# A MoE and attention kernel: half of the token blocks turned by VectorE in 32 by 32 squares

## The chip, the cores and the metric

The kernel runs on one core of a Trainium2 chip. The metric is the device time of one execution in microseconds (us). Before the change it is 405.93 us, the median of 3 runs.

## What is computed

x has 4 sequences of 512 tokens, 256 wide, float32: 2,048 tokens. It is normalised (xn), and the output is x plus attention(xn) plus a mixture of experts on xn:

```python
xn = _layernorm(x, axis=-1)
x = x + _L0_attn_ref(xn, Wq, Wk, Wv, Wo, bo) + _L0_ffn_ref(xn, router_w, router_bias, wg, wu, wd, swg, swu, swd)
# in _L0_ffn_ref, flat = xn as (2048, 256), E = 64 experts, F = 64, K = 4:
_, topk_idx = jax.lax.top_k(logits + router_bias, K)
g = jax.nn.silu(jnp.einsum('nd,edf->nef', flat, wg))
u = jnp.einsum('nd,edf->nef', flat, wu)
routed = jnp.einsum('ne,nef,efd->nd', comb, g * u, wd)
```

Each token goes to 4 of 64 experts; comb holds their weights. Two shared experts are added. Attention has 16 heads of 16 with a window of 64 and one key and value head.

## The kernel before, in words

Attention runs first, over NT = 16 tiles of 128 tokens, each engine with its own list of work written out by hand, tied by semaphores. In the meantime GpSimd scatters each normalised row to the HBM tensor `xs_d`, sorted by expert, once for each of its four experts (8,192 row slots). These are XB = 64 blocks of 128 rows of 256 numbers. With rounding to whole blocks per expert there are at most NBLK = 127 blocks of work, in NGRP = 32 groups of GS = 4; the blocks of work past 64 read token blocks that are already there, since a block of rows can hold several experts' rows.

The matmul with the expert weights needs a block with the features on the partitions. So each block b is loaded to one of NX = 8 buffers `xrow` (`load_block`, L1683 to L1691, a DMA of 128 rows of 1,024 bytes issued by SyncE), turned, and laid into `xall`, where it stays. Turning is `turn` on three engines:
- TensorE (L613 to L625): waits for the load and for a free bank, transposes two halves of the block (even and odd features, `c::NC`) into bank 0 or 4, and raises `g_T`.
- VectorE (L1139 to L1154) copies the even blocks from the bank to `xall`, and ScalarE (L874 to L889) the odd ones.

The first 10 blocks (FIRST) are turned in the last part of attention, at 177 to 195 us of the span. After that comes the loop over groups G = 1 to 32. `turns_of(G)` gives the blocks 4G + 6 to 4G + 9 in two pairs. TensorE's order in G is `ups(G)` (L650, 8 matmuls of a group's four blocks, each with its own wait for the weights and for the turned block), the first pair of turns (L624), `down(G-1)` (L675), the second pair. ScalarE does `silu(G)` (L896), a turn, `copy_y(G-1)` (L908, two copies), a turn. VectorE does a turn, `hidden(G)` (L1284, two products), a turn. GpSimd copies the picked weights (L1519, L1537).

SyncE's queue is in order. At T = 15 it issues the blocks 0 to 7, then two loads of the last eight experts, then (L1737 to L1745) blocks 8 and 9, a store of base (`store_base`, L1681), blocks 10 to 13, a store of base, and then down-weight loads (L1667) by turns with blocks 14 to 17. In G it issues for each block b of `turns_of(G)` the load of block b + 8, which waits until b's turn has read the buffer (L1690), and then `store_y(G-1)` (L1754), which waits for ScalarE's copy. In G = 1 the last store of base comes between the loads and the store of y, and a load of experts comes behind it in G = 1 and 2. ScalarE's `copy_y(1)` waits for all stores of base (L903), and from G = 2 on for the landing of the store of y of two groups before (L905). TensorE's `down(G)` waits for the copies of y of group G - 2 (L669).

At G = 17 (OTHER_DOWN) GpSimd begins to use two `xrow` buffers for weights, after all turns (L1529).

Of the kernel before, what the change touches and what calls it, by code (L numbers as in the profile page):

```python
# [17 lines left out]
B, L, D = 4, 512, 256  # L18
# [7 lines left out]
P = 128  # L26
NT = B * L // P
TPB = L // P
NC = D // P
# [115 lines left out]
def build(nc, x, Wq, Wk, Wv, Wo, bo, router_w, router_bias, wg, wu, wd, swg, swu, swd, c32, c16, edges, w32, w16, out):  # L145
# [4 lines left out]
    s = {n: ctx.enter_context(nc.semaphore("s_" + n)) for n in SEMAPHORES}  # L150
# [10 lines left out]
    bank = [psum[:, i * 512:(i + 1) * 512] for i in range(8)]  # L161
# [4 lines left out]
    xall = sb("xall", [P, NT * TOPK * D])  # L166
# [8 lines left out]
    xs_d = nc.dram_tensor("xs_d", (NT * P * TOPK, D), f32, kind="Internal").ap()  # L175
# [79 lines left out]
    NX, NW = 8, 4  # L255
# [18 lines left out]
    XB = NT * TOPK  # L274
# [46 lines left out]
    FIRST = 10  # L321
# [25 lines left out]
    up_bank_of = lambda G: bank[1 + G % 2]  # L347

    y_banks = lambda G: ((bank[3], bank[5]), (bank[6], bank[7]))[G % 2]
    turn_bank = lambda b: bank[4 * (b % 2)]  # L350

    turned = lambda b: (s["gT_dve"] if b % 2 == 0 else s["gT_out"], b // 2 + 1)

    turns_of = lambda G: [[b for b in range(4 * G + 6 + 2 * k, 4 * G + 8 + 2 * k) if b < XB] for k in range(2)]

# [4 lines left out]
    def tensor(pe):  # L360
# [251 lines left out]

        def turn(b):  # L613
            pe.wait_ge(s[f"xrow{b % NX}"], (b // NX + 1) * 16)
            if b >= 2:
                sem, n = turned(b - 2)
                pe.wait_ge(sem, n)
            elif b == 0:
                pe.wait_ge(s["max"], XT(NT - 1))
            else:  # L620
                pe.wait_ge(s["q_out"], 2 * NT)
            o = turn_bank(b)
            for c in range(NC):
                ins = pe.transpose(o[:, c * P:(c + 1) * P], xrow[b % NX][:, c::NC], ident)  # L624
            ins.then_inc(s["g_T"], 1)  # L625

        def turns(lo, hi):
            for b in range(lo, hi):
                turn(b)


        block_reg = [[ctx.enter_context(pe.register(f"block{n}_{i}")) for i in range(GS)] for n in range(2)]
# [136 lines left out]
        for G in range(1, NGRP + 1):  # L769
            if G == NGRP - 1:  # L770

                hidden(0, 0)
                down(G - 1)
            if G < NGRP:
                find(G)
                ups(G)
            if G == 1:
                project_out(NT - 1)
            for b in turns_of(G)[0]:
                turn(b)  # L780
            if G == NGRP:
                hidden(0, 1)
            if G != NGRP - 1:
                down(G - 1)
            for b in turns_of(G)[1]:
                turn(b)

        pe.wait_ge(s["with_x"], NT)
# [3 lines left out]
    def scalar(act):  # L792
# [79 lines left out]
                act.activation(th[i % 2], gate_bank(i), ACT.Tanh, scale=0.5).then_inc(s["th"], 1)  # L872

        def turn(b):  # L874
            if b == 1:

                act.wait_ge(s["q_left"], 2 * NT)
                act.wait_ge(s["weighted"], QB * (NT - 2))
            elif b == FIRST + 1:
                act.wait_ge(s["k_T"], NT)  # L880
                act.wait_ge(s["q_T"], 2 * NT)
                act.wait_ge(s["proj"], NT)
                act.wait_ge(s["weighted"], QB * NT)
            elif b in (SCORES_AT, SCORES_AT + 1):
                act.wait_ge(s["by_key"], XT(NT - 1))
                act.wait_ge(s["a_T"], NT)
                act.wait_ge(s["attended"], NT)
            act.wait_ge(s["g_T"], b + 1)
            act.activation(xall[:, b * D:(b + 1) * D], turn_bank(b)[:, 0:D], ACT.Copy).then_inc(s["gT_out"], 1)  # L889

        def silu(G):
# [93 lines left out]

        scores(NT - 1, 0, 0)
        scores(NT - 1, 0, 1)
        turn(1)
# [3 lines left out]
        turn(3)  # L992
        attention(NT - 2)
        turn(5)
        turn(7)
        silu(0)
        attention(NT - 1)
        turn(9)

        for G in range(1, NGRP + 1):  # L1000
            if G == NGRP - 1:
                copy_y(G - 1)
            if G < NGRP:
                silu(G)
            for b in turns_of(G)[0][1:]:
                turn(b)
            if G != NGRP - 1:
                copy_y(G - 1)
            for b in turns_of(G)[1][1:]:
# [7 lines left out]
    def vector(dve):  # L1017
# [119 lines left out]
            dve.tensor_tensor(ob, bank[7][:, 0:D], x_in[b][:, t, :], ALU.add).then_inc(s["with_x"], 1)  # L1137

        def turn(b):  # L1139
            if b == 0:  # L1140
# [4 lines left out]
            elif b == FIRST:  # L1145
                dve.wait_ge(s["q_T"], 2 * NT)
                dve.wait_ge(s["proj"], NT)
                dve.wait_ge(s["weighted"], QB * NT)
            elif b in (SCORES_AT, SCORES_AT + 1):
                dve.wait_ge(s["by_key"], XT(NT - 1))  # L1150
                dve.wait_ge(s["a_T"], NT)
                dve.wait_ge(s["attended"], NT)
            dve.wait_ge(s["g_T"], b + 1)
            dve.tensor_copy(xall[:, b * D:(b + 1) * D], turn_bank(b)[:, 0:D]).then_inc(s["gT_dve"], 1)  # L1154

        route_n = [0]

# [225 lines left out]
            if T > 1 and T < NT - 1:  # L1383
                add_x(T - 2)

        turn(0)
        add_x(NT - 3)
        tokens(NT - 2)
        turn(2)
        output(NT - 1)  # L1390
        turn(4)
        add_x(NT - 2)
        tokens(NT - 1)
        turn(6)
        hidden(0)
        turn(8)

        for G in range(1, NGRP + 1):
            if G == 1:
                add_x(NT - 1)  # L1400
            for b in turns_of(G)[0][:1]:
# [5 lines left out]
            for b in turns_of(G)[1][:1]:  # L1407
                turn(b)

        copy_last_y(NGRP - 1)  # L1410
# [23 lines left out]
    def gpsimd(pool):  # L1434
# [87 lines left out]
        def pick_down(G):  # L1522
            if G == 0:

                pool.wait_ge(s["max_T"], NT)
            elif G < OTHER_DOWN:
                pool.wait_ge(s["down"], 2 * G)
            elif G == OTHER_DOWN:
                pool.wait_ge(s["g_T"], XB)  # L1529
# [34 lines left out]
        slots = scatter()  # L1564
# [46 lines left out]
    def sync(sp):  # L1611
# [71 lines left out]
        def load_block(b):  # L1683
            if b == 0:
                sp.wait_ge(s["scattered"], NT * TOPK * 16)
                sp.wait_ge(s["gate"], 1)
            if b == NX // 2:
                sp.wait_ge(s["wslice"], 1)
            if b >= NX:
                sp.wait_ge(s["g_T"], b - NX + 1)  # L1690
            sp.dma_start(xrow[b % NX], xs_d[b * P:(b + 1) * P, :]).then_inc(s[f"xrow{b % NX}"], 16)  # L1691

        def load_blocks(lo, hi):
            for b in range(lo, hi):
# [127 lines left out]
```

## Time and profile before

| | us |
|---|---|
| median of 3 runs | 405.93 |
| lowest, highest | 404.23, 411.58 |
| span of the profiled execution | 407.3 |
| TensorE busy | 354.1 |
| VectorE busy | 248.5 |
| ScalarE busy | 189.3 |
| GpSimd busy | 257.5 |

The span runs from the first to the last instruction of one profiled execution. PE is TensorE's matmuls and PEld its weight loads, DVE is VectorE, ACT ScalarE, POOL GpSimd, SP SyncE; a q behind a name is the engine's sequencer, which waits and issues DMAs. A duration of a DMA instruction on SPq is the time that the queue was held by issuing it, not that of the transfer.

### The profile page before, as it was taken

Reading aid. Unit: us, or ns where it says so; the run is one execution under the profiler, and the core shown is the slowest. Engines: PE = TensorE matmul, PEld = TensorE weight load, DVE = VectorE, ACT = ScalarE, POOL = GpSimd, SP = SyncE. Lnnn points to the kernel's source line nnn. Section 1 sums busy time; section 2 is a strip of 40 time slices with the busy share of each in tenths; the row PEclk is TensorE's granted clock in tenths of the full one; section 3 lists DMA queues with packets and bytes.
Section 4 is the critical chain, followed back from the end, with each engine's and each line's share of the span. In section 5 each row is a group of like instructions: output and inputs, shape, how many; then the busy total and the mean of one; then the engine's idle time right before and its main releaser. Section 6 shows DMA issues by size and latency. Waiting matters only on the chain.

```text
span 407.3 us, 8670 instructions
## 1 busy us (share of the span) xinstructions
PE 354.1 (87%) x2711; PEld 259.3 (64%) x2711; DVE 248.5 (61%) x717; ACT 189.3 (46%) x359; POOL 257.5 (63%) x522
## 2 busy tenths in 40 slices
PE   6698487988976899899999999999999997989753
PEld 3696355665654556448889999999974544545442
DVE  4668877877876878624554645454444419375676
ACT  3485667686766677533455555555532111010100
POOL 5677986777777665022446566877837757667560
PEclk9969989898999889957999999999999999999969
DMA  8940144444484446545988873577974324434341
GB/s 255 213 109 1 54 131 146 131 146 133 161 241 150 142 146 176 156 141 134 296 263 269 267 249 132 181 244 233 337 252 120 105 85 129 128 94 129 103 129 52
DMA packets 73037, 66.81 MB, mean 164 GB/s; under 512 B 9054, under 2 KB 68702, under 8 KB 72994
## 3 DMA queue, kind: packets, MB, share of 16 engines
q1 hardware_dynamic: 66433, 49.30, 40.8%
q0 software_dynamic: 6144, 16.79, 13.0%
q8 instruction: 23, 0.38, 0.4%
q10 hardware_dynamic: 416, 0.18, 0.2%
q14 instruction: 21, 0.16, 0.1%
HBM read 36.78 MB, written 29.23 MB: 162 GB/s over the span
## 4 chain that ended last, share of the span: by engine, by line
PE 64%; DVE 15%; another core or an unknown queue 8%; issue 5%; ACT 4%; DMA 2%; POOL 1%; SPq 0%; DVEq 0%; ACTq 0%; POOLq 0%
PE bank L650 14%; PE bank L675 8%; PE bank L589 8%; PE bank L515 5%; PE bank L624 4%; PE bank L540 4%; PE bank L609 4%; DVE xall L1092 3%; PE bank L436 3%; PE bank L491 3%; DVE xall L1324 3%; PE bank L417 3%; PE bank L523 2%; PE bank L458 1%
## 5 line engine op out<-in xcount | busy, mean ns | idle before, releaser
L1500 POOL DMA_INDIRECT xs_d<-spare,slot_i x64 | 64.2, 1003 | 29.3 <-PE bank L515 7.5
L1593 POOL DMA_INDIRECT wall<-y_d,y_row x64 | 61.4, 959 | 33.7 <-issue 18.3
L1519 POOL COPY spare<-wall 128x256 f32 x127 | 46.9, 400 | 29.9 <-PE bank L650 18.0
L650 PE MATMUL bank<-xall,spare 128*128 x508 | 64.1, 279 | 0.2
L1284 DVE TENSOR_TENSOR spare<-bank,spare 64x512 f32<-64x512 f32 (+1 forms) x64 | 44.1, 690 | 31.0 <-ACT spare L896 30.1
L650 PEld LDWEIGHTS bank<-xall,spare 128*128 128x128 f32 x508 | 59.4, 192 | 2.8 <-issue 0.7
L589 PE MATMUL bank<-xnT,xall 128*128 128x512 f32 x128 | 57.7, 594 | 0.5 <-issue 0.5
L908 ACT ACTIVATE spare<-bank 128x512 f32<-128x512 f32 (+1 forms) x62 | 33.7, 593 | 29.5 <-PE bank L675 17.9
L847 ACT ACTIVATE xall<-bank 98x1024 bf16<-98x1024 bf16 x32 | 32.7, 1021 | 22.6 <-PE bank L436 14.5
L855 ACT ACTIVATE xall<-bank 128x512 f32<-128x512 f32 x64 | 36.6, 601 | 12.5 <-PE bank L491 7.4
L609 PE MATMUL bank<-xall 128*128 128x256 f32 x128 | 32.0, 400 | 11.6 <-DVE xall L1309 8.3
L589 PEld LDWEIGHTS bank<-xnT,xall 128*128 128x128 f32 x128 | 24.0, 190 | 26.1 <-issue 25.4
L872 ACT ACTIVATE xall<-bank 128x512 f32<-128x512 f32 x16 | 9.2, 596 | 66.7 <-remote 41.9
L609 PEld LDWEIGHTS bank<-xall 128*128 128x128 f32 x128 | 25.2, 201 | 21.8 <-DVE xall L1309 10.1
L491 PE MATMUL bank<-xall,wdn 128*128 128x256 bf16 x128 | 24.2, 285 | 13.2 <-ACT xall L855 5.6
L1324 DVE SCALAR_TENSOR_TENSOR xall<-wall,gate,xall 128x256 f32<-128x256 f32 x64 | 31.1, 487 | 2.3
L1154 DVE COPY xall<-bank 128x256 f32<-128x256 f32 x32 | 13.6, 425 | 28.7 <-PE bank L624 28.3
L896 ACT ACTIVATE spare<-bank 64x512 f32<-64x512 f32 (+1 forms) x32 | 18.8, 586 | 25.8 <-PE bank L650 25.7
L838 ACT ACTIVATE xall<-xall 128x768 bf16<-128x768 f32 (+2 forms) x48 | 28.8, 624 | 2.4 <-POOL xall L1490 1.8
L1092 DVE TENSOR_REDUCE xall<-bank 128x4 f32<-128x316 f32 x64 | 28.2, 478 | 1.1 <-PE bank L458 0.5
L1298 DVE SCALAR_TENSOR_TENSOR xall<-xall,bank 128x512 f32<-128x512 f32 x16 | 10.9, 681 | 23.0 <-ACT xall L872 21.2
L1537 POOL COPY small<-wdn 128x128 f32 x24 | 7.0, 293 | 27.7 <-PE bank L675 24.2
(172 smaller groups left out, 656.0 us busy)
## 6 DMA issues: line engine op xcount, KB each, us to landing
y_d<-spare SPq DMA_DIRECT2D x31, 512.0 KB, 4.1
wall<-in_wg SPq DMA_DIRECT2D x16, 256.0 KB, 4.8
wall<-in_wu SPq DMA_DIRECT2D x16, 256.0 KB, 5.0
wdn<-in_wd SPq DMA_DIRECT2D x16, 256.0 KB, 4.5
spare<-xs_d SPq DMA_DIRECT2D x32, 128.0 KB, 2.8
small<-xs_d SPq DMA_DIRECT2D x32, 128.0 KB, 3.3
wall<-in_x SPq DMA_DIRECT2D x4, 512.0 KB, 5.7
base_d<-spare SPq DMA_DIRECT2D x16, 128.0 KB
```

What stands on the lines that cost most here:

```text
L491: ins = pe.matmul(bank[2 + e][:, i * 256:(i + 1) * 256], kN[0:KROWS, near_of(T), u, :], qS[0:KROWS, T % NQ, u, :, :].rearrange("p h q -> p ...
L589: ins = pe.matmul((gate_bank(i), up_bank(i))[half], wsh[:, c, half, ex, f0:f0 + P], xnT[:, c, g * GN:(g + 1) * GN], start=c == 0, stop=c = ...
L609: ins = pe.matmul(shared_bank(T), hs[T // GT % 2][:, k, t * P:(t + 1) * P], wshd[:, k, :], start=k == 0, stop=k == FC - 1)
L650: ins = pe.matmul(up_bank_of(G)[:, j * P:(j + 1) * P], wcur[i % NW][:, c * 2 * F:(c + 1) * 2 * F], x_half[c][:, bass.ds(o, P)], start=c == ...
L855: act.activation(probs[n % 2][:, e * 512:(e + 1) * 512], bank[2 + e][:, :], ACT.Exp).then_inc(s["exp"], 1)
L908: act.activation(yb[G % 2][:, 0:n, half * P:(half + 1) * P], o[:, 0:n * P].rearrange("p (j d) -> p j d", d=P), ACT.Copy).then_inc(s["y_out ...
L1092: dve.tensor_reduce(maxf[T % 2][:, w * 8 + 4 * e:w * 8 + 4 * e + 4], bank[e][:, 0:4 * NEAR].rearrange("p (g n) -> p g n", g=4), AX.X, ALU.max,
L1284: ins = dve.tensor_tensor(hT[G % 2][half, 0:n], up_bank_of(G)[F:P, 0:n], sg[0:F, 0:n], ALU.mult)
L1324: dve.scalar_tensor_tensor(a, yk[:, T, k, :], gate[:, T, k:k + 1], a, ALU.mult, ALU.add).then_inc(s["sum"], 1)
L1500: pool.indirect_dma_start(out=xs_d, out_offset=bass.IndirectOffsetOnAxis(ap=slot_i[:, T, k:k + 1], axis=0), in_=x_n[b][:, t, :], in_offset ...
L1519: pool.tensor_copy(wcur[i % NW].rearrange("p (c g f) -> p c g f", c=NC, g=2), wall[:, bass.ds(o, WE)].rearrange("p (g c f) -> p c g f", c= ...
L1593: pool.indirect_dma_start(out=yk[:, T, k, :], out_offset=None, in_=of, in_offset=bass.IndirectOffsetOnAxis(ap=y_row[:, T, k:k + 1], axis=0 ...
```

## The change

Even blocks are turned by TensorE and copied by ScalarE. Odd blocks are turned by VectorE alone, which transposes squares of 32 by 32 from `xrow` to `xall`. Since a square's rows must be on the right 32 partitions already, an odd block is loaded by four DMAs, each to 32 partitions, in pieces of 256 bytes (64 numbers of one row): 4 x 128 pieces a block. VectorE's transpose reads `xrow` with a step of two numbers, so that even and odd features come apart. The buffer of an odd block is free when VectorE has turned it. The turns stand at the places in each engine's order where the copies stood, with even and odd exchanged; a bank is used by every second even block.

```diff
+    on_pe = lambda b: b % 2 == 0
+    turn_bank = lambda b: bank[4 * (b // 2 % 2)]
+    turned = lambda b: (s["gT_out"] if on_pe(b) else s["gT_dve"], b // 2 + 1)
+    SQ = 32
+    row_read = lambda b: (s["g_T"] if on_pe(b) else s["gT_dve"], b // 2 + 1)
+    row_loads = lambda b: 16 * (1 if on_pe(b) else P // SQ)
+    both_halves = lambda v: v.rearrange("p (c e h) -> p h c e", c=P // SQ, h=NC)
...
 # TensorE
         def turn(b):
             pe.wait_ge(s[f"xrow{b % NX}"], (b // NX + 1) * 16)
-            if b >= 2:
-                sem, n = turned(b - 2)
+            if b >= 4:
+                sem, n = turned(b - 4)
                 pe.wait_ge(sem, n)
...
-            for b in turns_of(G)[0]:
+            for b in turns_of(G)[0][:1]:
                 turn(b)
...
 # ScalarE
-            act.wait_ge(s["g_T"], b + 1)
+            act.wait_ge(s["g_T"], b // 2 + 1)
...
 # VectorE
-            dve.wait_ge(s["g_T"], b + 1)
-            dve.tensor_copy(xall[:, b * D:(b + 1) * D], turn_bank(b)[:, 0:D]).then_inc(s["gT_dve"], 1)
+            dve.wait_ge(s[f"xrow{b % NX}"], (b // NX + 1) * row_loads(b))
+            dve.transpose(xall[:, b * D:(b + 1) * D].rearrange("p (h c j) -> p h c j", h=NC, j=SQ),
+                          both_halves(xrow[b % NX])).then_inc(s["gT_dve"], 1)
...
 # SyncE
             if b >= NX:
-                sp.wait_ge(s["g_T"], b - NX + 1)
-            sp.dma_start(xrow[b % NX], xs_d[b * P:(b + 1) * P, :]).then_inc(s[f"xrow{b % NX}"], 16)
+                sem, n = row_read(b - NX)
+                sp.wait_ge(sem, n)
+            slots = xs_d[b * P:(b + 1) * P, :]
+            if on_pe(b):
+                sp.dma_start(xrow[b % NX], slots).then_inc(s[f"xrow{b % NX}"], 16)
+            else:
+                for a in range(P // SQ):
+                    of = slice(a * NC * SQ, (a + 1) * NC * SQ)
+                    sp.dma_start(xrow[b % NX][a * SQ:(a + 1) * SQ, :].rearrange("j (c n) -> j c n", n=NC * SQ),
+                                 slots.rearrange("(c j) d -> j c d", j=SQ)[:, :, of]).then_inc(s[f"xrow{b % NX}"], 16)
```

The numbers of the blocks in ScalarE's and VectorE's lists (`turn(1)`, `turn(0)` and so on) and in the waits ahead of the first ones are exchanged to match.

## Rows read from the trace of the kernel before

**Rows 1.** The page, busy time of each engine: us, share of the span, instructions.
```profile
PE 354.1 (87%) x2711; PEld 259.3 (64%) x2711; DVE 248.5 (61%) x717; ACT 189.3 (46%) x359; POOL 257.5 (63%) x522
```

**Rows 2.** The chain that ended last: start us, us, who, how many.
```profile
196.78 4.56 DMA base_d<-spare
...
232.34 1.09 PE bank L675 x16
233.44 0.68 PE bank L624 x4
...
236.38 1.09 PE bank L675 x16
...
249.59 1.98 PE bank L650 x16
...
289.55 1.98 PE bank L650 x16
...
292.62 1.98 PE bank L650 x16
```

**Rows 3.** Groups by line from 213 to 245 us: busy, mean ns; idle before.
```profile
L1284 DVE TENSOR_TENSOR spare<-bank,spare 64x512 f32<-64x512 f32 x16 | 11.1, 694 | 0.4
...
L1154 DVE COPY xall<-bank 128x256 f32<-128x256 f32 x16 | 6.8, 425 | 14.3 <-PE bank L624 14.1
L889 ACT ACTIVATE xall<-bank 128x256 f32<-128x256 f32 x16 | 6.1, 382 | 0.0
L624 PE MATMUL bank<-cf,spare 128*128 128x128 f32 x32 | 5.6, 296 | 0.0
```

**Rows 4.** Timeline of SyncE's queue: start us, us held, line, tiles, how many.
```profile
169.44 1.80 SPq L1691 DMA_DIRECT2D spare<-xs_d  x4
...
173.19 0.43 SPq L1621 DMA_DIRECT2D wall<-in_wg  x1
...
183.58 0.80 SPq L1691 DMA_DIRECT2D spare<-xs_d  x2
...
188.72 1.29 SPq L1667 DMA_DIRECT2D wdn<-in_wd  x2
...
196.78 0.43 SPq L1681 DMA_DIRECT2D base_d<-spare  x1
...
229.87 0.80 SPq L1691 DMA_DIRECT2D small<-xs_d  x2
230.71 0.43 SPq L1754 DMA_DIRECT2D y_d<-spare  x1
...
240.21 0.87 SPq L1691 DMA_DIRECT2D small<-xs_d  x2
```

**Rows 5.** DMA lines by source: ns min/median/max, first and last start; L1691's landing.
```profile
L1691 SPq DMA_DIRECT2D spare<-xs_d x32: 319/430/951, 169.4 to 236.9; - x32
DMA to landing us min/median/max: 2.0/3.2/5.3
...
L1613 SPq DMA_DIRECT2D wall<-in_x x4: 447/502/602, 0.7 to 4.5; - x4
...
L1770 SPq DMA_DIRECT2D xall<-base_d x4: 507/528/817, 283.5 to 292.1; - x4
...
L1667 SPq DMA_DIRECT2D wdn<-in_wd x16: 608/642/1812, 108.5 to 191.8; - x16
...
L1629 SPq DMA_DIRECT2D xall<-in_Wk x1: 694/694/694, 2.5 to 2.5; - x1
```

**Rows 6.** DMA queues, packets, MB, share: ScalarE's (page), SyncE's (213 to 244 us).
```profile
q10 hardware_dynamic: 416, 0.18, 0.2%
...
q1 hardware_dynamic: 8476, 8.06, 82.5%
```

**Rows 7.** Engines busy by stretch; last: granted clock, DMA share, GB/s.
```profile
174.00:188.00 14.00, 14.00 (x63) 7.85 (x64) 3.76 (x9) 4.98 (x10) 1.14 (x5) 0.52 0.41 122
...
213.00:245.00 32.00, 31.98 (x314) 29.98 (x316) 17.33 (x32) 17.88 (x40) 19.34 (x64) 1.00 0.84 265
```

More of the change, by code:

```diff
@@ L349, in build @@
     y_banks = lambda G: ((bank[3], bank[5]), (bank[6], bank[7]))[G % 2]
-    turn_bank = lambda b: bank[4 * (b % 2)]
-    turned = lambda b: (s["gT_dve"] if b % 2 == 0 else s["gT_out"], b // 2 + 1)
+    on_pe = lambda b: b % 2 == 0
[5 more added lines that the diff above has]
+    both_halves = lambda v: v.rearrange("p (c e h) -> p h c e", c=P // SQ, h=NC)
     turns_of = lambda G: [[b for b in range(4 * G + 6 + 2 * k, 4 * G + 8 + 2 * k) if b < XB] for k in range(2)]
@@ L628, in turns @@
             for b in range(lo, hi):
-                turn(b)
+                if on_pe(b):
+                    turn(b)
         block_reg = [[ctx.enter_context(pe.register(f"block{n}_{i}")) for i in range(GS)] for n in range(2)]
@@ L784, in tensor @@
                 down(G - 1)
-            for b in turns_of(G)[1]:
+            for b in turns_of(G)[1][:1]:
                 turn(b)
@@ L874, in turn @@
         def turn(b):
-            if b == 1:
+            if b == 0:
                 act.wait_ge(s["q_left"], 2 * NT)
+                act.wait_ge(s["k_T"], NT)
                 act.wait_ge(s["weighted"], QB * (NT - 2))
-            elif b == FIRST + 1:
+            elif b == FIRST:
                 act.wait_ge(s["k_T"], NT)
@@ L987, in scalar @@
         scores(NT - 1, 0, 1)
-        turn(1)
+        turn(0)
         scores(NT - 1, 1, 0)
@@ L991, in scalar @@
         act.activation(unread[:, :], ident[:, 0:1], ACT.Silu)
-        turn(3)
+        turn(2)
         attention(NT - 2)
-        turn(5)
-        turn(7)
+        turn(4)
+        turn(6)
         silu(0)
         attention(NT - 1)
-        turn(9)
+        turn(8)
         for G in range(1, NGRP + 1):
@@ L1004, in scalar @@
                 silu(G)
-            for b in turns_of(G)[0][1:]:
+            for b in turns_of(G)[0][:1]:
                 turn(b)
@@ L1008, in scalar @@
                 copy_y(G - 1)
-            for b in turns_of(G)[1][1:]:
+            for b in turns_of(G)[1][:1]:
                 turn(b)
@@ L1139, in turn @@
         def turn(b):
-            if b == 0:
+            if b == 1:
                 dve.wait_ge(s["q_part"], 3 * NT)
@@ L1144, in turn @@
                 dve.wait_ge(s["weighted"], QB * (NT - 2))
-            elif b == FIRST:
+            elif b == FIRST + 1:
                 dve.wait_ge(s["q_T"], 2 * NT)
@@ L1384, in vector @@
                 add_x(T - 2)
-        turn(0)
+        turn(1)
         add_x(NT - 3)
         tokens(NT - 2)
-        turn(2)
+        turn(3)
         output(NT - 1)
-        turn(4)
+        turn(5)
         add_x(NT - 2)
         tokens(NT - 1)
-        turn(6)
+        turn(7)
         hidden(0)
-        turn(8)
+        turn(9)
         for G in range(1, NGRP + 1):
@@ L1400, in vector @@
                 add_x(NT - 1)
-            for b in turns_of(G)[0][:1]:
+            for b in turns_of(G)[0][1:]:
                 turn(b)
@@ L1406, in vector @@
                 hidden(G)
-            for b in turns_of(G)[1][:1]:
+            for b in turns_of(G)[1][1:]:
                 turn(b)
@@ L1528, in pick_down @@
             elif G == OTHER_DOWN:
-                pool.wait_ge(s["g_T"], XB)
+                pool.wait_ge(s["g_T"], XB // 2)
+                pool.wait_ge(s["gT_dve"], XB // 2)
             else:
@@ L1689, in load_block @@
             if b >= NX:
-                sp.wait_ge(s["g_T"], b - NX + 1)
-            sp.dma_start(xrow[b % NX], xs_d[b * P:(b + 1) * P, :]).then_inc(s[f"xrow{b % NX}"], 16)
+                sem, n = row_read(b - NX)
+                sp.wait_ge(sem, n)
+            slots = xs_d[b * P:(b + 1) * P, :]
+            if on_pe(b):
+                sp.dma_start(xrow[b % NX], slots).then_inc(s[f"xrow{b % NX}"], 16)
[4 more added lines that the diff above has]
+                                 slots.rearrange("(c j) d -> j c d", j=SQ)[:, :, of]).then_inc(s[f"xrow{b % NX}"], 16)
         def load_blocks(lo, hi):
```

## The prediction

> **What bounds the kernel now.** I read the page first: TensorE is busy for 87% of the span, so the first guess is that less work for TensorE is less time [rows 1]. The changed part is a small stretch, so I went to the chain that ended last. From 205 us to 249 us it is a strict round of TensorE lines, L675, L624, L650, L624, and one group of four blocks takes 236.38 - 232.34 = 4.04 us. From 249 us on, when all 64 blocks are turned, the same round without L624 takes 292.62 - 289.55 = 3.07 us [rows 2]. So TensorE sets the pace there, and four turned blocks cost it 0.97 us, 0.24 us each. The granted clock is 1.00 in this stretch (2.4 GHz) [rows 7].
>
> Then I asked who is next. In 213 to 245 us a VectorE copy L1154 takes 425 ns and a ScalarE copy L889 382 ns; both engines are mostly idle beside them [rows 3]. SyncE's queue issues everything else: per group four block loads (L1691) and one store of y (L1754). A pair of loads holds it 0.80 us, the store 0.43 us [rows 4], so about 2.1 of 4.04 us. The DMA engines are the busiest after TensorE: 0.84 of the same stretch [rows 7]. Both have little room, and the change puts work on just these two.
>
> **The change, part by part.**
>
> TensorE loses 32 of 64 turns: per group 2 x 0.24 = 0.49 us, which would make the round 3.55 us if TensorE stayed the bound.
>
> ScalarE does the same 32 copies as before, only of other blocks: nothing. Bank use is the same two banks with the same two turns between uses: nothing.
>
> VectorE exchanges 32 copies of 425 ns for 32 transposes of 256 elements per partition. Before shows no VectorE transpose. Below I take the copy's 0.43 us; it has the same element count. Above I let it grow until it would matter: VectorE's other work in a group is the 1.4 us of L1284 (two of 694 ns) [rows 3], so two transposes could take 2.2 us each before they filled the round of 5.8 us that comes out below. It isn't the bound at any value I believe.
>
> The DMA engines: the packets of 1,024 bytes take 0.825 x 16 x 31 us / 8476 = 48 ns each [rows 6]. A group moves 1,024 of them now. After, it moves 768 of them and 1,024 of 256 bytes. For these the nearest row is the ScalarE queue's 416 packets of 0.18 MB in all, 0.2% of 16 engines' 407.3 us, so about 31 ns each (24 to 39 by the rounding), taken where little else ran [rows 6]; the upper end is the 48 ns of a big one. Per group: (768 x 48 + 1024 x 31)/16 = 4.3 us, at the ends 3.8 and 5.4 us. So already the transfers alone would take back the 0.49 us. The Trainium skill (DMA: Bandwidth & Descriptors, Specifications) says the same from the other side: transfers under 512 bytes don't run at line rate. The trace has no load of 256-byte pieces beside full traffic that would test it.
>
> SyncE's queue: this is the step that decides. An odd block is now four DMAs, 128 in all where there were 32. Eight block loads in a row took 173.19 - 169.44 us = 3.75 us, so 0.47 us from one issue to the next, though the queue waited for nothing; a single one after a pause takes 0.32 us [rows 4, 5]. What a piece (32 partitions, three dimensions, 32 KB) costs the queue isn't in the trace. Below: 0.37 us, the shortest load plus the 0.05 us between issues. Above: 0.73 us, from the 0.69 us of L1629 [rows 5]. Between them stand the loads whose SBUF side is contiguous and whose DRAM side has three dimensions, as here: L1613 median 0.50 us, L1770 0.53 us, L1667 0.64 us [rows 5]. I take 0.51 + 0.04 = 0.55 us per piece, since L1613 and L1770 are nearest in layout. For all else 0.47 us.
>
> A group's issues then take 2 x 0.47 + 8 x 0.55 + 0.47 = 5.81 us, over TensorE's 3.55, the DMA engines' 4.3 and the 4.04 of before. The queue becomes the bound. Now in order of time, with each issue at its price:
> - From 169.44 us: blocks 0 to 7, 4 x 0.47 + 16 x 0.55 = 10.7 us, to 180.1; two expert loads, to 181.1; blocks 8 and 9, 2.67 us, to 183.7; a store of base, to 184.2. Blocks 1, 3, 5 and 7 still come before their turn, since the turns run from 178 to 189 us.
> - Blocks 10 to 13, 5.34 us, to 189.5 (their turns free the buffers from 183.58 on); the store of base to 190.0; two pairs of down-weight loads (1.29 us and a gap of 0.05 each [rows 4]) and blocks 14 to 17 (5.34 us), to 198.0; blocks 18 to 21, to 203.4.
> - The last store of base, to 203.8. It was issued at 196.78 us, and its landing is 4.56 us of the chain, since ScalarE's copy of y for group 1 waits for it [rows 2, 4]. It is 6.7 us late.
> - One expert load and the store of y, to 204.8; group 2, 5.34 + 0.94, to 211.1; groups 3 to 11, 9 x 5.81 = 52.3, to 263.4; in group 12 only blocks 62 and 63, 2.67, to 266.0. In before this last pair began at 240.21 [rows 4].
> - The last piece, issued at 265.5, lands 3.2 us later [rows 5], VectorE turns it in 0.43 us, and TensorE may use block 63 at 269.1 us. It used it three quarters into the run that began at 249.59, at 251.1 [rows 2]. That is 18.0 us late, after all turning is done. From there the round has no turn in it and is the one of before, so nothing is given back.
>
> Queued behind the slow issues are the stores of y; a store late keeps ScalarE from writing the buffer two groups on, ScalarE keeps TensorE from the banks. By the sums above this delay is about the same as that of the last block, so it isn't added.
>
> Sum: 0 for ScalarE, VectorE and the DMA engines (all under 5.81 us per group), TensorE's gain hidden, +18.0 us for the queue. The profiled execution spans 407.3 us; the median of the runs is 405.93, 1.4 us less, and I know nothing else around the span. 407.3 + 18.0 is 425.3 in that execution; 405.9 + 18.0 = 424 us for the median. I leave out the clock: in 174 to 188 us it was granted 0.52, after TensorE had gone idle for short times [rows 7], and here TensorE would be idle 2.3 us of every 5.8. At half speed its round is 7.1 us. It could cost some us more, a reason for a long upper side.
>
> **Rivals.**
> - *Faster, the other side.* The pieces are issued in under 0.27 us each; then 3 x 0.47 + 8 x 0.27 = 3.55 us, the queue keeps up, and if the small packets take no more engine time than their bytes (1,024 x 12 ns, a quarter of 48), the round falls to 3.55 us for 12 groups: 12 x 0.49 = -5.9 us, and five of the ten early turns, 5 x 0.24 = -1.2 us: 399 us. Against it: no issue in the trace is under 0.32 us. The Trainium skill leans this way (DMA: Bandwidth & Descriptors, Issuing engines are not separate DMA queues): the sequencer's time for a DMA is usually small beside the DMA. Here the row of eight loads shows 0.47 us each. Chance 0.05.
> - *The queue about keeps up, the DMA engines set the pace.* A piece costs 0.37 to 0.45 us. At 0.37 the last piece comes in time by the same sum, and the 4.3 us of the DMA engines over 10 groups are +2.6 us, less what the eight buffers lend: 404 to 411 us. Chance 0.13.
> - *Forecast: the queue bounds, pieces at 0.45 to 0.70 us.* Each 0.01 us of a piece is 128 x 0.01 = 1.3 us. At 0.47: 415 us (1 us of the gain goes into waits for turns). At 0.68, by L1667: 441 us. Chance 0.75.
> - *Worse.* Pieces at 0.73 us, 447 us, or TensorE at half clock for most of the stretch. Chance 0.07.
> - *A slow transpose:* over 2.2 us it would add to the round; nothing speaks for it. The Trainium skill (VectorE: DVE Perf Modes, The three transpose paths) has VectorE's blocks quicker than TensorE's turn. It would add nothing to the sum. It is inside the 0.07.
>
> **How the numbers follow.** About 2% can be told from no change here, 398 to 414 us. Faster by more: 0.05. Within: 0.13. Slower: 0.82. The range goes from 411 (the upper end of the second rival, leaving out it and the first) to 442 (L1667's price, leaving out the worst): 0.8.
>
> **What would show it.** SyncE's queue waiting for nothing from 185 to 265 us, L1691 with 160 issues (128 of them near 0.5 us); the round of L650 to L650 near 5.8 us with idle time of TensorE ahead of L624 and L650; the last base store issued near 203 us; L1154's place taken by a transpose near 0.43 us; the DMA share under 0.8. I am wrong if pieces cost the queue under 0.45 us, if idle waits of L1691 for turns remain, or if the round is bound by packets.

## The result, and the profile after

The changed kernel is slower, by the sign and inside the range that were forecast, and 10 us beyond the likeliest value.

| | before | after |
|---|---|---|
| median of 4 runs, side by side on one chip | 408.12 us (404.23 to 411.58) | 434.4 us (431.62 to 437.2) |
| ratio of the comparison | | 1.0721, 95% interval 1.0642 to 1.0801 |
| profiled execution | span 407.3 us | 437.2 us, span 435.9 us |

(The ratio compares runs in the chip's faster state alone, so it isn't the quotient of the medians, which is 1.064; the same goes for the ratios below.) Against the forecast of 424 us the median is 10.4 us up.

Lines have moved: L650 is now L657, L675 is L682, L624 is L630, and L1691 is split. Even blocks are issued at L1704, the pieces of odd blocks at L1709. VectorE's copy of L1154 is the transpose of L1162, the store of y is L1773, the store of base L1691.

The page of the changed kernel: busy time of each engine, and the shares of the chain that ended last.

```profile
PE 352.8 (81%) x2647; PEld 255.7 (59%) x2647; DVE 250.8 (58%) x717; ACT 188.7 (43%) x359; POOL 258.1 (59%) x522
...
PE 34%; SPq 16%; DVE 16%; another core or an unknown queue 11%; issue 9%; ACT 6%; DMA 5%; POOL 1%; DVEq 0%; ACTq 0%; POOLq 0%
SPq L1709 11%; PE bank L657 7%; PE bank L682 4%; PE bank L595 3%; DVE xall L1333 3%; PE bank L521 3%; SPq L1704 3%; PE bank L442 3%; DMA spare<-xs_d 2%; PE bank L615 2%; DMA small<-xs_d 2%; PE bank L546 2%; PE bank L423 2%; ACT xall L845 2%
```

TensorE has 64 instructions fewer than in [rows 1] and loses only 1.3 us of busy time. The engine totals barely move, so they don't tell where 28.6 us of span come from. The chain does: SyncE's queue, which had 0% of it in the kernel before, has 16%, and 11% of the span is the single line L1709 that issues the pieces.

The timeline of SyncE's queue after (start us, us held, line, tiles, how many), at the first load, around the last store of base, for one group of four blocks and for the last pair:

```profile
172.15 0.38 SPq L1704 DMA_DIRECT2D spare<-xs_d  x1
...
205.98 0.43 SPq L1691 DMA_DIRECT2D base_d<-spare  x1
...
206.93 0.57 SPq L1773 DMA_DIRECT2D y_d<-spare  x1
...
245.53 0.50 SPq L1704 DMA_DIRECT2D small<-xs_d  x1
246.08 2.42 SPq L1709 DMA_DIRECT2D small<-xs_d  x4
248.55 0.43 SPq L1704 DMA_DIRECT2D spare<-xs_d  x1
249.02 1.85 SPq L1709 DMA_DIRECT2D spare<-xs_d  x4
250.92 0.43 SPq L1773 DMA_DIRECT2D y_d<-spare  x1
251.40 0.50 SPq L1704 DMA_DIRECT2D spare<-xs_d  x1
...
269.37 0.50 SPq L1704 DMA_DIRECT2D small<-xs_d  x1
269.91 2.43 SPq L1709 DMA_DIRECT2D small<-xs_d  x4
```

Read it against [rows 4]. The sum of the durations and the 0.05 us between issues fill the time: from 245.53 to 251.40 the queue is without an instruction for no more than these gaps, and that is the new round, 5.87 us where it was 4.04. The last pair begins at 269.37 us where it began at 240.21.

The source view of the pieces (durations ns min/median/max), against [rows 5]:

```profile
L1709 SPq DMA_DIRECT2D spare<-xs_d x64: 317/432/1851, 172.6 to 266.0; - x64
L1709 SPq DMA_DIRECT2D small<-xs_d x64: 429/432/1692, 177.3 to 271.9; - x64
...
  DVE xall L1162: 44.7, 22
```

The source view of the transpose, against the copy in [rows 3]:

```profile
L1162 DVE STREAM_TRANSPOSE xall<-spare x16: 433/445/447, 178.4 to 267.9; 128x256 f32<-128x256 f32 x16
```

The third line of the first view says who waited for the pieces: VectorE's transposes, 44.7 us in all. VectorE is quick enough (445 ns); it stands and waits for its data.

The engines by stretch after (length; busy us and count of PE, PEld, DVE, ACT, POOL; last the granted clock, the DMA engines' busy share, GB/s), against [rows 7]:

```profile
174.00:188.00 14.00, 12.21 (x92) 7.55 (x90) 3.69 (x9) 6.82 (x14) 3.96 (x12) 1.00 0.57 153
188.00:213.00 25.00, 18.38 (x129) 16.75 (x130) 10.70 (x21) 7.46 (x18) 8.38 (x26) 0.80 0.65 162
213.00:265.00 52.00, 38.09 (x329) 32.57 (x328) 19.41 (x35) 17.73 (x42) 22.87 (x73) 0.96 0.62 176
```

TensorE is now busy for 38 of 52 us, and the DMA engines are at 0.62 where they were at 0.84. Nothing but the queue is full. ScalarE's copies of y (L916, L908 before) waited in these 52 us for stores of y to land, 30.3 us in all (busy, mean ns; idle before):

```profile
L916 ACT ACTIVATE spare<-bank 128x512 f32<-128x512 f32 x16 | 8.7, 595 | 30.3 <-DMA y_d<-spare 30.3
```

That is not a second bound: the stores stand in the same queue behind the pieces, and the queue itself never waited more than 0.4 us for a copy or a turn.

The chain after (start us, us, who, how many), from the landing of the last piece:

```profile
271.91 3.17 DMA small<-xs_d
...
278.06 1.98 PE bank L657 x16
...
281.13 1.98 PE bank L657 x16
```

Once block 63 is in, the round is 281.13 - 278.06 = 3.07 us, the same as in [rows 2]. The run of L657 that starts at 278.06 is the one that started at 252.66 before (249.59 + 3.07). So 25.4 us are lost by here.

### The profile page after: what moved, and what is told of

Same layout as the page of the kernel before. It is cut to its first block, busy times and chain, and to the rows that moved or that the text cites. A ratio compares the mean times of both kernels' runs of the same rounds, so it can differ in the third digit from the quotient of the medians.

```text
span 435.9 us, 8608 instructions
## 1 busy us (share of the span) xinstructions
PE 352.8 (81%) x2647; PEld 255.7 (59%) x2647; DVE 250.8 (58%) x717; ACT 188.7 (43%) x359; POOL 258.1 (59%) x522
## 4 chain that ended last, share of the span: by engine, by line
PE 34%; SPq 16%; DVE 16%; another core or an unknown queue 11%; issue 9%; ACT 6%; DMA 5%; POOL 1%; DVEq 0%; ACTq 0%; POOLq 0%
SPq L1709 11%; PE bank L657 7%; PE bank L682 4%; PE bank L595 3%; DVE xall L1333 3%; PE bank L521 3%; SPq L1704 3%; PE bank L442 3%; DMA spare<-xs_d 2%; PE bank L615 2%; DMA small<-xs_d 2%; PE bank L546 2%; PE bank L423 2%; ACT xall L845 2%
## 5 line engine op out<-in xcount | busy, mean ns | idle before, releaser
L657 PE MATMUL bank<-xall,spare 128*128 x508 | 68.7, 291 | 1.5 <-issue 0.4
L657 PEld LDWEIGHTS bank<-xall,spare 128*128 128x128 f32 x508 | 63.1, 202 | 5.5 <-issue 3.3
L1293 DVE TENSOR_TENSOR spare<-bank,spare 64x512 f32<-64x512 f32 (+1 forms) x64 | 43.9, 685 | 33.9 <-ACT spare L904 33.3
L916 ACT ACTIVATE spare<-bank 128x512 f32<-128x512 f32 (+1 forms) x62 | 33.6, 593 | 63.6 <-DMA y_d<-spare 42.5
L615 PE MATMUL bank<-xall 128*128 128x256 f32 x128 | 32.9, 408 | 13.3 <-issue 8.7
L442 PE MATMUL bank<-cb,xall 128*98 128x128 bf16 x256 | 21.3, 230 | 0.2 <-ACT xall L854 0.2
```

Of the source, the lines that this page charges most:

```text
L442: ins = pe.transpose(o[0:SROWS + MROWS, h, :], qrow[T % 2][:, 8 * i + h, :], identb)
L615: ins = pe.matmul(shared_bank(T), hs[T // GT % 2][:, k, t * P:(t + 1) * P], wshd[:, k, :], start=k == 0, stop=k == FC - 1)
L657: ins = pe.matmul(up_bank_of(G)[:, j * P:(j + 1) * P], wcur[i % NW][:, c * 2 * F:(c + 1) * 2 * F], x_half[c][:, bass.ds(o, P)], start=c == ...
L1293: ins = dve.tensor_tensor(hT[G % 2][half, 0:n], up_bank_of(G)[F:P, 0:n], sg[0:F, 0:n], ALU.mult)
```

## The experiments

A result is the ratio to the kernel before with its 95% interval. The chips differ: the kernel before takes 373.8 and 373.4 us on the chips of the first eight runs (four each) and 407.8 us on that of the last four. Each ratio is against runs of the kernel before on the same chip.

The first question was what of the change costs: the number of issues, the small packets, or both.

**e1_split: only the issues.** The kernel before, with odd blocks loaded by four DMAs of 32 whole rows. No small packets, and TensorE still turns all blocks.

```diff
-            sp.dma_start(xrow[b % NX], xs_d[b * P:(b + 1) * P, :])...
+                for a in range(4):
+                    sp.dma_start(xrow[b % NX][32 * a:32 * a + 32, :],
+                                 xs_d[b * P + 32 * a:b * P + 32 * a + 32, :])...
```

> The kernel before, but each odd block is loaded by four DMAs of 32 whole rows (1,024-byte pieces); TensorE turns all blocks as before. So it has the number of issues of the change (160 for 64 blocks) and nothing else of it. Theory 'queue' (SyncE's queue is held 0.47 us by each issue): a group takes 11 issues, 5.2 us, and about 0.5 us more around the store of y as in the changed kernel, so 5.7 to 5.9 us a round where it was 4.04; +24 to +30 us, ratio 1.06 to 1.075. Rival 'packets' (256-byte pieces fill the DMA engines or land late): there are none, so the ratio is 0.99 to 1.01. Rival 'VectorE' (the transpose holds the buffers): also 0.99 to 1.01.

Measured: 400.82 us against 373.81, ratio 1.0748 (1.0688 to 1.0808). SyncE's queue in this kernel, timeline:

```profile
212.86 0.42 SPq L1759 DMA_DIRECT2D y_d<-spare  x1
213.33 0.50 SPq L1692 DMA_DIRECT2D small<-xs_d  x1
213.87 2.35 SPq L1695 DMA_DIRECT2D small<-xs_d  x4
216.26 0.42 SPq L1692 DMA_DIRECT2D spare<-xs_d  x1
216.73 1.83 SPq L1695 DMA_DIRECT2D spare<-xs_d  x4
218.61 0.42 SPq L1759 DMA_DIRECT2D y_d<-spare  x1
```

The round is 218.61 - 212.86 = 5.75 us, and the pattern is the one of after: 1.83 us for four issues, and 2.35 us for the four behind a store of y. So a loss of the change's size appears without a single small packet and without VectorE, and a piece's hold (0.42 us here, with 32 packets; 0.43 in the change, with 128 packets and three dimensions) doesn't come from its layout.

**e2_small: only the small packets.** The kernel before, with each odd block in one DMA of 256-byte pieces, each from another row than its neighbour.

```diff
+                sp.dma_start(xrow[b % NX].rearrange("p (c n) -> p c n", c=4),
+                             bass.AP(v.tensor, v.offset, [[D, P], [D + 64, 4], [1, 64]]))...
```

> The kernel before, but each odd block is loaded by one DMA of 512 pieces of 256 bytes (to 128 partitions; the pieces of a row come from neighbouring rows, so the odd blocks' data are mixed up and the output is not the reference's). It has the change's small packets and not its issues. Theory 'queue': 64 issues as before, ratio 0.995 to 1.015; the round stays at 4.04 us or goes to at most 4.3 us if the small packets cost the engines 31 ns. Rival 'packets': most of the loss is here, ratio over 1.04.

Measured: 1.0037 (0.9992 to 1.0083). The windows of this kernel:

```profile
190.00:220.00 30.00, 29.97 (x300) 27.97 (x299) 17.06 (x31) 16.36 (x38) 17.12 (x57) 1.00 0.90 261
```

and the source view of its small load:

```profile
L1696 SPq DMA_DIRECT2D spare<-xs_d x16: 362/434/828, 155.3 to 218.9; - x16
```

One DMA of 512 packets is held for 434 ns, as one of 128 packets is. What comes behind it is held a little longer, 0.51 us for the store of y here against 0.43 in the changed kernel:

```profile
195.91 0.43 SPq L1696 DMA_DIRECT2D small<-xs_d  x1
196.38 0.51 SPq L1760 DMA_DIRECT2D y_d<-spare  x1
```

The DMA share goes up to 0.90, and TensorE stays full. So small packets alone cost nothing that can be told from zero here.

**e3_plain: the gain without its price.** The changed kernel with plain loads of whole blocks, which leaves out putting each square on its 32 partitions. It shows what VectorE's half of the turns is worth when the loads come in time.

```diff
-    row_loads = lambda b: 16 * (1 if on_pe(b) else P // SQ)
+    row_loads = lambda b: 16
...
+            sp.dma_start(xrow[b % NX], slots).then_inc(s[f"xrow{b % NX}"], 16)
```

> The changed kernel with each odd block loaded by one plain DMA of whole rows; VectorE transposes what lies there, so the output is not the reference's (the squares of the odd blocks are at the wrong places). It has the change's work on the engines without its loads. Theory 'queue': SyncE has 64 issues, TensorE sets the round at 3.55 us, or the DMA engines at about 3.4; -4 to -8 us, ratio 0.98 to 0.99. Rival 'VectorE' (transposes or the exchanged order of turns hold the loop): slower than before, ratio over 1.02. Rival 'packets' says the same as 'queue' here.

Measured: 0.9767 (0.9714 to 0.982), a bit more than expected. Its chain:

```profile
199.70 1.09 PE bank L682 x16
...
203.26 1.09 PE bank L682 x16
```

and its windows:

```profile
180.00:212.00 32.00, 32.00 (x323) 29.75 (x323) 19.02 (x36) 20.20 (x46) 21.03 (x70) 1.00 0.99 323
```

The round is 203.26 - 199.70 = 3.56 us; the forecast's working had 3.55. That the DMA engines would be busy 0.99 of the time and still keep up had not been expected.

**e4_pairs: the same layout with fewer issues.** Blocks are taken in pairs: 4q and 4q+1 come in one DMA and TensorE turns them, 4q+2 and 4q+3 come in four DMAs that carry the pieces of both. Six issues a group with the store of y, not eleven, and VectorE still does half the turns.

```diff
+    on_pe = lambda b: b % 4 < 2
...
+            slots = xs_d[(b - 1) * P:(b + 1) * P, :]
+            if on_pe(b):
+                sp.dma_start(to(0, P).rearrange("p (i d) -> p i d", i=2), ...)
+            else:
+                for a in range(P // SQ):
+                    sp.dma_start(to(a * SQ, (a + 1) * SQ).rearrange("j (c n) -> j c n", n=NC * SQ),
+                                 slots.rearrange("(c j) d -> j c d", j=SQ)[:, :, of])...
```

> A correct kernel with the change's 256-byte pieces and VectorE's transposes, but half of the issues: blocks 4q and 4q+1 are TensorE's and come in one DMA, blocks 4q+2 and 4q+3 are VectorE's and come in four DMAs of 32 partitions and eight pieces each. A group has 6 issues where the changed kernel has 11. Theory 'queue': 6 x 0.47 + 0.5 = 3.3 us is under TensorE's 3.55 us and near the DMA engines' 3.6 us, so the round is 3.6 to 3.9 us; the time is -1 to -6 us against before, ratio 0.985 to 1.0. Rival 'packets': as many small packets as the change, so still at least half of its loss, ratio over 1.03.

Measured: 0.9978 (0.9937 to 1.0019). The loss of 7% is gone, and there is no gain that can be measured. Its windows:

```profile
180.00:212.00 32.00, 30.16 (x295) 27.42 (x293) 16.40 (x31) 18.41 (x44) 20.55 (x67) 1.00 0.95 267
```

and two pieces of its chain, with the turn of TensorE that the first one held up (in brackets its idle time before it):

```profile
175.41 5.71 DMA base_d<-spare
...
198.08 3.23 DMA spare<-xs_d
```

```profile
182.71 0.76 PE L632 MATMUL bank<-cf,small 128*128 128x128 f32 x4 [0.87 <-ACT xall L897]
```

The chain passes through the last store of base and, later, through two block loads. But TensorE had other work for most of that time: it was idle for 0.87 us at the store of base and for 32.00 - 30.16 = 1.8 us in the whole window. The DMA engines, at a share of 0.95, have little slack. From the first load to silu of group 14, the last with turns, it is 72.2 us here and 65.3 in e3; no run takes these 7 us apart.

**e5_base: take away that wait.** e4 with the last store of base issued ahead of the loads of blocks 18 to 21.

```diff
+            if G == 1:
+                store_base(NT - 1)
             for bs in turns_of(G):
...
-            if G == 1:
-                store_base(NT - 1)
```

> e4_pairs with the last store of base issued ahead of the loads of blocks 18 to 21 instead of behind them. In e4 TensorE stood still for about 5 us for the landing of this store. Theory 'queue': the store is issued about 2 us earlier, so -1 to -3 us against e4; ratio to the kernel before 0.988 to 0.997. Rival 'landing' (the DMA engines are full there, so it lands no earlier): as e4, 0.998.

Measured: 0.9962 (0.9923 to 1.0002), not to be told from e4. The 5 us of standing still in the expectation were read from the chain; TensorE's own idle time at that store was 0.87 us (above), so little was to be had.

**e6_y_on_act: one issue less a group, and none behind a store.** The changed kernel, with the stores of y issued by ScalarE.

```diff
+                act.dma_start(y_d[(G - 1) * GS * P:((G - 1) * GS + n) * P, :].rearrange("(j p) d -> p j d", p=P),
+                              yb[(G - 1) % 2][:, 0:n, :]).then_inc(s[f"y{(G - 1) % 2}"], 16)
...
-            store_y(G - 1)
+            if G - 1 >= NGRP - 2:
+                store_y(G - 1)
```

> The changed kernel with the stores of y (all but the last two) issued by ScalarE behind its copies and turns. The number of issues and packets is that of the change, but SyncE has 10 of a group's 11. Theory 'queue' (one sequencer's queue is the bound): the round goes from 5.87 to 4.7 to 5.0 us, and the ratio to before from 1.07 to 1.03 to 1.05. Rival 'shared' (what makes descriptors, or the DMA engines, is the bound for both queues together): no gain, over 1.06.

Measured: 1.0754 (1.0686 to 1.0822), a miss. SyncE's queue in this kernel; ScalarE issued a store of y at 219.43 and held 0.37 us for it:

```profile
216.79 1.89 SPq L1714 DMA_DIRECT2D spare<-xs_d  x4
218.73 0.43 SPq L1709 DMA_DIRECT2D spare<-xs_d  x1
219.20 3.66 SPq L1714 DMA_DIRECT2D spare<-xs_d  x4
```

The four pieces at 219.20 held the queue 3.66 us in place of 1.86, next to a store that another queue issued; one of the four was held 2.23 us. The same is seen within 1.4 us of nearly every store. So the extra hold goes with the store of y, not with its place in SyncE's queue. Ten groups of loads took 56.0 us here and 61.8 in the changed kernel, so the round is 5.6 us and not the 4.7 to 5.0 expected. The trace shows where part of the 5.8 us went. From the first load to silu of group 14 it is 93.8 us here and 101.3 in the changed kernel; from there to the last silu 58.6 against 55.3, because ScalarE waited for stores of y to land, as in this piece of the chain:

```profile
265.67 5.91 DMA y_d<-spare
```

So about 4 us are left of the gain inside the trace. The total doesn't show them, but the changed kernel was not run on this chip, and 4 us are 1.1% of its time, within what the intervals of e6 and e12 leave open.

**e7_two and e10_uneven: how many issues fit.** The kernel before, with odd blocks in two DMAs: 64 + 64 rows (e7), then 32 + 96 rows (e10). Seven issues a group.

```diff
+                for a in range(2):
+                    sp.dma_start(xrow[b % NX][64 * a:64 * a + 64, :],
+                                 xs_d[b * P + 64 * a:b * P + 64 * a + 64, :])...
```

> e1_split with two DMAs of 64 whole rows for each odd block instead of four of 32. 7 issues a group. Theory 'queue': 7 x 0.47 + 0.5 = 3.8 us is just under TensorE's 4.04 us, so nearly all of e1's loss is gone: ratio 1.00 to 1.015. Rival 'any split costs' (a loss in proportion to the added issues, 3 to 1 against e1): 1.02 to 1.03.

```diff
+                for lo, hi in ((0, 32), (32, 128)):
+                    sp.dma_start(xrow[b % NX][lo:hi, :], xs_d[b * P + lo:b * P + hi, :])...
```

> e7_two with its two DMAs cut as 32 and 96 rows instead of 64 and 64. The same 7 issues a group. In e7 the DMAs to 64 partitions held the queue 0.60 us, those to 128 or 32 partitions 0.43 to 0.45 us. If the partition count made e7 slower than forecast: issues near 0.45 us, 7 x 0.47 + 0.5 = 3.8 us a group, ratio 1.00 to 1.012. Rival 'in proportion to the added issues': as e7, 1.02 to 1.03.

Measured: e7 1.0243 (1.0177 to 1.0308), a miss; e10 0.9999 (0.9944 to 1.0055). The source view of e7's loads:

```profile
L1695 SPq DMA_DIRECT2D spare<-xs_d x32: 444/597/1407, 155.0 to 227.3; - x32
```

two rows of its queue:

```profile
205.11 1.09 SPq L1695 DMA_DIRECT2D spare<-xs_d  x2
206.24 0.59 SPq L1759 DMA_DIRECT2D y_d<-spare  x1
```

and the source view of e10's loads:

```profile
L1695 SPq DMA_DIRECT2D spare<-xs_d x32: 421/429/1452, 169.7 to 235.8; - x32
```

In e7 an issue behind a DMA to 64 partitions is held 0.58 to 0.60 us at the median, whatever it is: the second half of a block, an even load (0.58), the store of y (0.59). The first half, behind an even load, takes 0.46 at the median. So the time goes with the DMA issued before. Behind one to 32 or 96 partitions it is 0.43. With three issues of a group behind an even load or a store and four behind a half, the round of e7 is about 4.6 us: from store of y to store of y it is 206.24 - 201.67 and 210.99 - 206.24, 4.57 and 4.75 us.

In e10 the expected 3.8 us a round was too low. The stores of y from 199.70 to 238.32 us are 4.3 us apart on average, because most groups have one load held about 1 us and some two. Between its first and last load the queue waited 4.5 us, where it waited 28 in the kernel before. So with seven issues the queue is all but full, and in the loop even a little slower than TensorE's 4.04 us; yet the time is that of before within 0.6%. Loads that run ahead of their turns would explain it; that isn't shown. From the first load to silu of group 14 it is 74.4 us, against 72.2 in e11 on the same chip, so a small loss may be there. The threshold lies here: the queue's sum, long holds included, against the round of the engine that sets the pace.

**e8_best: all that looked good together.** e5 with the stores of y on ScalarE.

> e5_base and e6's change together: pairs of blocks, the store of base first, the stores of y by ScalarE. SyncE has 5 issues a group, 2.4 us. Theory 'queue': the queue is no bound any more; TensorE (3.55 us) or the DMA engines (about 3.6 us) set the round; ratio to before 0.975 to 0.99. Rival 'packets': e4 was already held by the DMA engines, so this is no faster than e5, 0.988 to 1.0. Rival 'ScalarE' (its issues delay silu): slower than e5.

Measured: 1.0014 (0.9975 to 1.0053), a miss. From the first load to silu of group 14 it is 71.4 us, and 71.7 in e5. So five issues a group leave room in the queue, and there is no gain where the turns are: the queue isn't what holds this layout back. Against e5, on the same chip, it is even 0.6% slower (means 373.5 and 371.4 us), as the rival 'ScalarE' said, though not by delaying silu. Its chain, after the turns:

```profile
240.09 6.68 DMA y_d<-spare
...
252.86 8.83 DMA y_d<-spare
```

As in e6, ScalarE waits there for stores of y that it issued itself; TensorE was idle behind these two for 0.4 and 2.5 us.

**e9_one_small: what the small packets take of the gain.** e3 with the odd blocks in one DMA of 256-byte pieces as in e2.

> e3_plain (VectorE turns half of the blocks, one DMA a block) with the odd blocks' loads in 256-byte pieces as in e2_small, still one DMA each. The pieces come from neighbouring rows, so the output is not the reference's. Everything of the change but its 96 added issues. Theory 'queue': as e3, 0.977, up to 0.985 for the packets' engine time. Rival 'packets take the gain' (the DMA engines were 0.95 busy in e3's round of 3.56 us, and a small packet costs 23 to 31 ns): the round goes to 3.8 to 4.0 us, ratio 0.99 to 1.0.

Measured: 0.9869 (0.9814 to 0.9924), between the two expectations. Its windows:

```profile
200.00:240.00 40.00, 39.86 (x397) 36.84 (x398) 25.67 (x46) 23.74 (x56) 26.61 (x88) 1.00 1.01 295
```

and from its chain:

```profile
218.27 5.52 DMA small<-xs_d
```

The round is 3.56 us for long stretches. The chain holds one load for 5.52 us, but TensorE ran on beside it: it was busy 39.86 of these 40 us. From the first load to silu of group 14 it is 67.1 us here and 65.3 in e3. By the ratios small packets take 1.0% of VectorE's 2.3% (0.9869 against 0.9767); that is rough, since each has 0.6% to either side and the two ran on different chips.

**e11_before_base: the base store alone, on the kernel before.**

> The kernel before with the last store of base issued ahead of the loads of blocks 18 to 21. Correct. If SyncE's order alone held ScalarE's copy of y there: -1 to -2.5 us, ratio 0.993 to 0.998. Rival (the store lands as late, behind the other transfers): 0.998 to 1.002.

Measured: 1.0047 (1.0000 to 1.0094), no gain: a miss. The 4.56 us of [rows 2] were in the chain, but TensorE had other work meanwhile. In the kernel before it stood idle for 0.42 us behind that wait:

```profile
202.93 0.48 PE L624 MATMUL bank<-cf,spare 128*128 128x128 f32 x2 [0.42 <-ACT xall L889]
```

Its two runs of L675 around the wait start 4.99 us apart (198.35 and 203.34), the same two in e11 4.28 us (192.03 and 196.31). So about 0.7 us was to be had, less than these runs can tell.

**e12_after: the change once more, beside e9 to e11.**

> The changed kernel itself once more, on the chip of the other experiments, to have e1_split and e6_y_on_act beside it. Theory 'queue': as e1_split within 1%, since both have 160 issues: ratio 1.065 to 1.08. Rival 'packets' or 'VectorE': over e1_split by more than 1%, or under it by as much as VectorE's help for TensorE (e3, 2.3%).

Measured: 440.19 us against 407.81, 1.0749 (1.0658 to 1.0841). With e3 and e9 the account is: VectorE's help -2.3%, small packets about +1.0%, the 96 added issues +8.8%. The last is what remains (1.0749 - 0.9869 = 0.088), and e3 ran on another chip than e9 and e12. Alone, on the kernel before, the issues cost +7.5% (e1).

## Why the prediction was right, and where it was off

**The bound** was named rightly. The round of the issues was forecast at 5.81 us and is 5.87; the queue has at most 0.4 us without an instruction at any time between 172 and 272 us; the base store went out at 205.98 us where 203.4 was forecast from a start 2.7 us earlier. e1 shows the mechanism alone.

**The price of a piece** was mis-sized: 0.432 + 0.04 = 0.47 us, not 0.55. I had taken the nearest layouts (L1613, L1770 in [rows 5]) over the nearest row of the same kind, the eight loads in a row at 0.47. Over 128 pieces that is 128 x 0.08 = 10 us too much. What made up for it I had left out: in nearly every group one load is held 0.5 us longer, a few 1 us and more, in sum 12 us over the median for all 160 loads. In the round shown above four pieces behind a store take 2.42 us, and four others 1.85. Eight pieces at 0.55 make 4.4 us; measured, 2.42 + 1.85 + 0.09 = 4.36. The round came out right by two errors that cancel, which is luck. The trace of before had such long loads too (the maximum of 951 ns in [rows 5]); at a median I passed over them. The forecast had called pieces under 0.45 us a sign of being wrong. The time held, 0.432, is under that; the time from issue to issue, which its sum uses, is 0.47, and with the long holds all issues together average 0.55.

**From the first load to the store of y0** 35.4 us were forecast (204.8 - 169.44); measured 207.50 - 172.15 = 35.35. **From there to the last pair** the forecast had 58.6 us, and it took 61.9 (207.50 to 269.37): three rounds of 7.2, 6.5 and 6.2 us in place of 5.87 are 2.4 us of the 3.3. **The last piece** was issued 2.5 us after its pair began (2.1 forecast), landed 3.17 us later (3.2) and was turned in 0.45 us (0.43).

**The stores of y.** The forecast named ScalarE's wait for them and didn't add it. The wait came (30.3 of 52 us), and the sum was right to leave it out, since it comes from the same queue.

**The start** was 2.7 us later: the first load came at 172.15, not 169.44. The program up to there is the same. Where the kernel before takes about 408 us, the three kernels with the changed order of turns (after, e9, e12) began at 171.2 to 172.2 us, the three with the old one (before, e10, e11) at 168.8 to 169.4. On the two faster chips there is no such split: 151.9 to 155.7 and 153.4 to 154.9. I have no cause.

**The end.** At the run of L657 at 278.06 the loss is 25.4 us, which is 18.0 + 2.7 (start) + 3.3 (long rounds) + 0.4 (last pieces) + 1.0 (a wait for VectorE's L1293 behind them). The forecast gave nothing back and added nothing after that point; the spans differ by 28.6 us, so 3.2 us more are lost in the tail. The windows of the tail, after:

```profile
370.00:407.00 37.00, 35.00 (x105) 19.65 (x106) 18.79 (x38) 2.87 (x6) 23.59 (x26) 1.00 0.37 111
407.00:436.00 29.00, 13.74 (x49) 10.68 (x48) 21.37 (x45) 1.09 (x3) 11.24 (x12) 0.75 0.31 91
```

and before, for the same last 28 us:

```profile
379.00:407.00 28.00, 14.85 (x53) 10.89 (x52) 19.71 (x41) 1.68 (x3) 11.82 (x12) 0.86 0.30 93
```

The clock was granted at 0.75 there, against 0.86. Part of those 3.2 us may be that; no run takes it apart, so it stays open. From the last silu to the end it is 103.9 us in before, 107.2 in after and 111.6 in e12, but 89.6 to 90.6 in all eight traces of the faster chips, e1 among them, whose turns end as late as the change's (silu of group 14 is 100.4 us behind the first load, in after 101.3). So late turns alone don't lengthen the tail.

**TensorE's gain, hidden.** Right: 3.56 us in e3. **The DMA engines** were priced high. A 256-byte packet was put at 31 ns (24 to 39). In 213 to 265 us the queue's packets, MB and share of 16 engines are:

```profile
q1 hardware_dynamic: 16929, 9.07, 61.8%
```

They took 0.618 x 16 x 52 us = 514 us. The kept trace has each packet with its size and time: 6,481 of 1,024 bytes took 52 ns on average, 8,474 of 256 bytes 17 ns, 1,462 of 4 bytes 9 ns and 512 of 512 bytes 28 ns. In e9, with the DMA engines full, a 256-byte packet took 18 ns. A group then costs the DMA engines (768 x 52 + 1,024 x 17)/16 = 3.6 us where 4.3 was forecast, in either case under the queue's 5.87. The Trainium skill (DMA: Bandwidth & Descriptors, Specifications) asks for at least 512 bytes for line rate. The trace agrees in direction: a quarter of the bytes took a third of the time. In this kernel it didn't decide.

**VectorE's transpose** was 0.445 us where 0.43 was taken. The rival of a slow transpose falls. **The half clock** came in short stretches: TensorE was granted 0.80 in 188 to 213 us, where before had 1.00, and 0.96 in 213 to 265 us; in 174 to 188 us, where before was granted 0.52, after had 1.00. The queue was full through all of it, so nothing of the loss in the rounds is put down to the clock, and the caution for a long upper side was not needed. The 0.52 does belong to the comparison: from the first load to silu of group 14 the trace of before took 78.6 us, that of e11 (clock 1.00 there) 72.2, so against a trace without it the loss would probably be more than the 28.6 us of span.

**The rivals.** The faster one needed issues under 0.27 us; the shortest of 128 pieces took 0.317. The Trainium skill (DMA: Bandwidth & Descriptors, Issuing engines are not separate DMA queues) calls the sequencer's time to start a DMA "usually small relative to the DMA itself". As a ratio that holds here: a piece takes 2.0 us from issue to landing and 0.47 us of an in-order queue. It doesn't help, though: landings overlap while issues don't, and here the small number decides. The second rival, in which the queue about keeps up, had the right condition and nearly the right price: at 0.45 us a piece and no long issues it might have come true. e4, e8 and e9 show its world, with the DMA engines at 0.95 to 1.07, and there the change is worth between nothing and 1.3%.

## What to carry to other kernels

Price a DMA by its issue as well as by its bytes: here each one took about 0.47 us of an in-order queue, whether it brought 32 KB or 128 KB, and seven a group were all that the loop of 4.04 us could take without a loss. Before splitting transfers to suit another engine's layout, add up the queue's round and set it beside the round of the engine in front; up to there a split costs nothing that the runs can tell (e10), beyond it the added issues lengthen the round (e1, e7). And a chain that names a wait tells what ended last, not how long the engine stood still: look at the engine's own idle time before removing the wait (4.56 us in the chain and 0.42 us idle in e11's case, 5.71 and 0.87 in e4, 5.52 and nothing in e9).

## What the runs showed of the hardware that was not expected

- The time an issue is held goes with the DMA issued just before it. Medians behind a DMA to 32, 96 or 128 partitions in up to 128 packets are 0.42 to 0.46 us (e1, e7, e10, after); behind 512 packets, the store of y or the 256-byte load of a whole block, 0.50 to 0.51 (e2, after; in e9, with the DMA engines full, 0.64 for the load that follows); behind 64 partitions 0.58 to 0.60 (e7), also for an even load and the store of y.
- Behind a 512-KB store of y one of the next loads is held about 0.5 us longer (0.94 in place of 0.43 in after), in every kernel with split loads, and also when another queue issued the store (e6). In e6 the longest such group of four was 3.66 us in place of 1.86.
- VectorE's transpose of 128 x 256 f32 in 32 x 32 squares, reading every second column, took 445 ns, 5% more than the plain copy of the same shape from a bank (425 ns).
- Chips differ by 34 us for the same kernel (373.8 and 407.8 us), but not in the rounds: 4.04 us with turns and 3.07 without on both. The first load comes at 152 to 156 us on the faster ones and at 169 to 172 on the slower, and from the last silu to the end it takes 90 to 91 us on the ones and 104 to 112 on the other, after as well as before.
